# A two-layer sequence kernel: the scan stage's products in parts of two passes, new slot tables, and the conditioning work inside layer 0 of the first batch

## The reference

```
# layer 0: linear attention, 16 heads of 32, masked keys and values
q, k, v = LN(x) @ Wq, Wk, Wv;  q = softmax(q over features);  k = softmax(k over tokens)
y = q @ (k^T v)
scale, shift = silu(c) @ film_emb_W + film_emb_b          # 8x1024 @ 1024x1024
x = x + silu(LN(y) * (1 + scale) + shift) @ film_out_W
# layer 1: attention and a state-space scan side by side
shift, scale, gate = silu(c) @ W_ada + b_ada              # 8x1024 @ 1024x1536
xm = LN(x) * (1 + scale) + shift
attn = softmax attention(xm), 8 heads of 64, @ Wproj
xr, z = xm @ W_in;  u = silu(causal conv of xr, 4 taps)
dt, Bm, Cm = u @ W_x;  delta = softplus(dt @ W_dt)
h = exp(delta * A) * h + delta * u * Bm  (16 states, 1024 channels, over 512 tokens);  y = sum(h * Cm)
ssm = ((y + u * D) * silu(z)) @ W_out
out = x + gate * silu(LN([ssm, attn]) @ W_full + b_full)
```

## Time and profile before

| | us |
|---|---|
| median of 3 runs | 3960.05 (3959.69 to 3961.09) |
| the profiled execution's own time | 3962.71 |
| its span | 3960.8 |
| `setup` up to the next block's first instruction | 75.21 |
| layer 0 and attention, all batches, and the scan stage's first front | to the first scan at 1621.50 |
| 16 halves, of 140.3 (first) and 146.4 (second) in the middle | 1627.20 to 3876 |
| the last tail | to 3960.8 |

### The profile page before, as it was taken

The page is one execution under the profiler, slowest core; times in us unless marked ns, Lnnn a source line. Parts: engine busy times, 40 slices in busy tenths (PEclk is TensorE's granted clock), DMA queues, the critical chain, the costliest instruction groups (busy, mean ns, idle before and its releaser), DMA issues.

```text
span 3960.8 us, 36362 instructions
## 1 busy us (share of the span) xinstructions
PE 3387.0 (86%) x12362; PEld 1788.0 (45%) x12362; DVE 2718.3 (69%) x3459; ACT 2029.8 (51%) x3486; POOL 1893.9 (48%) x1139
## 2 busy tenths in 40 slices
PE   4899999999999998769888878888888888888758
PEld 1444444444444433444544544544544444544443
DVE  1344435344443533699898898997997997998992
ACT  1234343343433433846755755755765766676542
POOL 0021222212122211867667767766767766766661
PEclk8999999999999999668898898898898898888859
DMA  5001010100101010112122131222132122221111
GB/s 204 35 1 46 1 45 1 46 28 18 46 1 45 1 75 31 46 32 78 64 91 83 58 111 59 85 96 72 61 99 70 65 95 72 66 92 61 41 61 43
DMA packets 100937, 230.04 MB, mean 58 GB/s; under 512 B 10305, under 2 KB 10417, under 8 KB 97682
## 3 DMA queue, kind: packets, MB, share of 16 engines
q1 hardware_dynamic: 97186, 220.50, 16.5%
q10 hardware_dynamic: 3568, 7.21, 0.5%
HBM read 193.85 MB, written 33.83 MB: 57 GB/s over the span
## 4 chain that ended last, share of the span: by engine, by line
PE 18%; POOL 14%; DVE 14%; issue 13%; ACT 3%; DMA 0%; POOLq 0%; SPq 0%; DVEq 0%; ACTq 0%
POOL HS L1144 10%; PE bank L1505 10%; DVE HS L1383 6%; DVE acc L1388 5%; PE bank L1581 4%; PE bank L1522 3%; PE bank L1579 1%; DVE U L1420 1%; POOL delta L1159 1%; POOL ZS L1150 1%; ACT bank L1221 1%; POOL DU L1162 1%; POOL comb L1175 1%; PE bank L1531 0%; DVE G L1408 0%
## 5 line engine op out<-in xcount | busy, mean ns | idle before, releaser
L1144 POOL TENSOR_TENSOR HS<-DU,brep 128x1024 f32<-128x1024 f32 x512 | 1196.6, 2354 | 635.8 <-PE bank L1522 635.8
L1383 DVE TENSOR_TENSOR_SCAN HS<-bank,HS 128x1024 f32<-128x1024 f32 x512 | 1169.2, 2284 | 70.6 <-ACT bank L1221 58.0
L1522 PE MATMUL bank<-ident,HS 128*128 128x128 f32 x4096 | 686.8, 319 | 340.4 <-DVE acc L1388 305.4
L1221 ACT ACTIVATE bank<-delta,aneg 128x511 f32<-128x511 f32 x1024 | 662.0, 680 | 500.7 <-DVE HS L1383 498.6
L1522 PEld LDWEIGHTS bank<-ident,HS 128*128 128x128 f32 x4096 | 558.4, 164 | 616.3 <-DVE HS L1383 399.9
L446 POOL TENSOR_TENSOR PR<-PR,rrec 128x512 f32<-128x512 f32 x256 | 260.0, 1039 | 1128.6 <-DVE rrec L691 1128.6
L1388 DVE SCALAR_TENSOR_TENSOR acc<-bank,C,acc 128x512 f32<-128x512 f32 x960 | 668.4, 740 | 134.0 <-PE bank L1522 132.4
L1505 PE MATMUL bank<-XM,w_l 128*128 128x512 f32 x1024 | 499.8, 636 | 43.9 <-DVE U L1420 19.1
L1505 PE MATMUL bank<-w_l,G 128*128 128x512 f32 x1024 | 474.4, 609 | 7.3 <-ACT delta L1231 3.9
L523 ACT ACTIVATE PR<-bank,nsmax 128x512 f32<-128x512 f32 x256 | 173.5, 682 | 374.4 <-DVE nsmax L687 374.4
L757 PE MATMUL bank<-w_l,NT 128*128 128x512 f32 x768 | 342.6, 595 | 5.1 <-ACT NT L477 5.1
(11 more groups left out here) (169 smaller groups left out, 3877.8 us busy)
## 6 DMA issues: line engine op xcount, KB each, us to landing
brep<-b_d SPq DMA_DIRECT2D x256, 256.0 KB, 3.2
w_l<-in_L_cond_W_in SPq DMA_DIRECT2D x14, 2048.0 KB, 9.7
w_l<-in_L_cond_W_full SPq DMA_DIRECT2D x8, 2048.0 KB, 8.6
w_l<-in_L_cond_W_out SPq DMA_DIRECT2D x7, 2048.0 KB, 9.0
X<-in_x SPq DMA_DIRECT2D x8, 1024.0 KB, 5.2
x_d<-X SPq DMA_DIRECT2D x8, 1024.0 KB, 4.6
xm_d<-XM SPq DMA_DIRECT2D x8, 1024.0 KB, 3.9
ot_d<-OT SPq DMA_DIRECT2D x8, 1024.0 KB, 5.8
```

Source lines behind the costliest of these rows:

```text
L1144: nc.gpsimd.tensor_tensor(HS[:, u % DEEP], DU[:, chunks(j, s), :], brep[:, m % 3, :].unsqueeze(1).to_broadcast([P, UC, T]), ALU.mult).then ...
L1221: last = nc.scalar.activation(dA[:, s, i, 1:T], delta[:, c, 1:T], ACT.Exp, scale=aneg[:, c, n:n + 1])
L1383: nc.vector.tensor_tensor_scan(h, dA[:, u % 2].rearrange("p i t -> p (i t)"), h, 0.0, ALU.mult, ALU.add).then_inc(scanned, 1)
L1522: last = nc.tensor.transpose(y_bank[t % 2][:, i * P:(i + 1) * P], h, ident[:])
```

## The change

One part: `setup` is gone. Its loads, products and row arithmetic stand in `attend`; the first load is now X. The two conditioning weights come in five pieces of 2 MB, which lie in rooms that layer 1 uses later; `conditioning(g)` issues their products, adds and turns after chosen half-steps of batch 0's layer 0. Weights are waited for one by one. GpSimd's copy of a batch's row of `per_batch` is gone; the row is read in place.

The other part: in `mix` each product is taken up in parts of two matmuls, each with a slot of its own in tuples (`PE_XR = ((0, 0), (2, 2), ...)`: both parts of x0 at slot 0, of x1 and of x2 at slot 2), and all tables have new numbers.

```diff
-            setup(nc, a, bank, ident, cols, bq8, aneg, convw, per_batch, gate_d, X, load, arrived)
-            attend(nc, a, bank, ident, cols, col, bq8, per_batch, x1_d, xm_d, ot_d, X, W, load, load_wide, arrived)
+            attend(nc, a, bank, ident, cols, col, bq8, aneg, convw, per_batch, gate_d, x1_d, xm_d, ot_d, X, W, load, load_wide, arrived)
...
+        room = [PR[:, 0].rearrange("p e t k -> p (e t k)"), PR[:, 1].rearrange("p e t k -> p (e t k)"), QK.rearrange("p i c t -> p (i c t)"),
+                wqkv.rearrange("p c n -> p (c n)")[:, 0:EC * D]]
+        piece = [room[j % 4].rearrange("p (c n) -> p c n", n=D) for j in range(5)]
...
+        row_bank, turn_bank = bank[6:8], (bank[5], bank[4])
...
+        PE_PIECE, PE_ROWS = (14, 15, 19, 20, 21), (18, 26)
+        DVE_PIECE, DVE_ROWS = (15, 16, 20, 21, 22), (19, 27)
...
+        def l0_alone(l0, conditioning=None):
             for g in range(SLOTS):
-                l0(n, g)
+                l0(0, g)
+                if conditioning:
+                    conditioning(g)
...
+                def load_piece(j):
+                    w, k = ("L0_cond_film_emb_W", j) if j < 2 else ("L1_cond_W_ada", j - 2)
+                    sp.dma_start(piece[j], a[w][:, k * D:(k + 1) * D].rearrange("(c p) n -> p c n", p=P)).then_inc(piece_in[j], 16)
+
+                sp.dma_start(X[:], a["x"][0].rearrange("(t p) d -> p t d", p=P)).then_inc(x_in, 16)
+                for name, first, n in VECTORS:
+                    src = a[name][first:first + n * P].rearrange("(c p) -> c p", p=P)
+                    sp.dma_start(vecrows[COL[name]:COL[name] + n, :], src).then_inc(vec_in, 16)
+                sp.dma_start(maskrows[:], a["mask_BxS_ik0"].rearrange("b (t p) -> (b t) p", p=P)).then_inc(rows_in, 16)
                 load_mask(0)
+                for name in ("L0_cond_Wk", "L0_cond_Wq", "L0_cond_Wv"):
+                    load(sp, name).then_inc(arrived[name], 16)
+                load_piece(0)
+                load_piece(1)
+                load(sp, "L0_cond_film_out_W").then_inc(arrived["L0_cond_film_out_W"], 16)
+                load_piece(2)
+                load_piece(3)
+                sp.wait_ge(cond_mm, 1)
+                load_piece(4)
+                sp.wait_ge(cond_mm, 4)
+                load(sp, "L1_cond_Wqkv").then_inc(arrived["L1_cond_Wqkv"], 16)
+                sp.wait_ge(rows_done, 5)
+                sp.dma_start(gate_d, rows[4]).then_inc(gate_out, 16)
...
-                    if n:
-                        pool.wait_ge(*r0.done(n - 1, "x1", DC - 1))
-                    nc.gpsimd.tensor_copy(cur[:], per_batch[:, n, :]).then_inc(cur_done, 1)
...
+                def conditioning(g):
+                    for j in at(DVE_PIECE, g):
+                        dve.wait_ge(cond_mm, j + 1)
+                        nc.vector.tensor_tensor(rows[j], row_bank[j % 2][0:B, :], rows[j], ALU.add).then_inc(rows_done, 1)
+                    for i in at(DVE_ROWS, g):
+                        sc, sh, at_a, at_b, gain, shift, done = (
+                            (0, 1, FILM_A, FILM_B, "L0_cond_film_norm_scale", "L0_cond_film_norm_bias", film_done),
+                            (1, 0, LN1_A, LN1_B, "L1_cond_ln1_g", "L1_cond_ln1_b", ln1_done))[i]
+                        dve.wait_ge(rows_turned, i + 1)
+                        y = turn_bank[i][:, 0:2 * DC * B].rearrange("p (k c b) -> p k c b", k=2, b=B)
+                        link(nc.vector.tensor_scalar(scale1[:, i], y[:, sc], 1.0, None, ALU.add))
+                        for first, v in ((at_a, gain), (at_b, shift)):
+                            for c in range(DC):
+                                last = nc.vector.tensor_scalar(per_batch[:, :, first + c], scale1[:, i, c, :], col(v, c), None, ALU.mult)
+                        link(last)
+                        dst = per_batch[:, :, at_b:at_b + DC].rearrange("p b c -> p c b")
+                        link(nc.vector.tensor_tensor(dst, dst, y[:, sh], ALU.add))
+                        nc.vector.memset(spare[:], 0.0).then_inc(done, 1)
...
+                def conditioning(g):
+                    for j in at(PE_PIECE, g):
+                        if j == 0:
+                            pe.wait_ge(condT_done, 1)
+                        pe.wait_ge(piece_in[j], 16)
+                        if j >= 2:
+                            pe.wait_ge(rows_done, j - 1)
+                        for c in range(EC):
+                            last = nc.tensor.matmul(row_bank[j % 2][0:B, :], condT[:, c, :], piece[j][:, c, :], start=(c == 0), stop=(c == EC - 1))
+                        last.then_inc(cond_mm, 1)
+                    for i in at(PE_ROWS, g):
+                        pe.wait_ge(rows_done, 2 * i + 2)
+                        for k in range(2 * DC):
+                            src = (film, ada)[i][:, k * P:(k + 1) * P]
+                            last = nc.tensor.transpose(turn_bank[i][:, k * B:(k + 1) * B], src, ident[0:B, 0:B])
+                        last.then_inc(rows_turned, 1)
...
+        SPARED = ((), ())
...
-        PE_XR = {0: 0, 1: 1, 2: 2, 4: 3, 5: 4, 6: 5, 8: 6, 9: 7}
-        PE_Z = {10: 0, 11: 1, 14: 2, 20: 3, 22: 4, 23: 5, 25: 6, 26: 7}
-        PE_XD = {12: 0, 13: 1}
-        PE_DT1, PE_C = {15: 0, 16: 1, 18: 2, 19: 3}, 17
-        PE_O = {1: (0, 0), 2: (0, 1), 5: (1, 0), 6: (1, 1), 14: (2, 0), 15: (2, 1), 20: (3, 0), 21: (3, 1)}
-        PE_P1, PE_P0 = {29: 0, 30: 1, 31: 2}, {0: 3}
-        PE_CT = {10: (0, 0), 11: (0, 1), 16: (1, 0), 17: (1, 1), 22: (2, 0), 23: (2, 1), 27: (3, 0), 28: (3, 1)}
-        PE_F = {12: (0, 0), 13: (0, 1), 18: (1, 0), 19: (1, 1), 24: (2, 0), 25: (2, 1), 29: (3, 0), 30: (3, 1)}
-        ACT_Z = {12: 0, 14: 1, 16: 2, 23: 3, 25: 4, 26: 5, 28: 6, 29: 7}
-        ACT_P1, ACT_P0 = {30: 0, 31: 1}, {0: 2, 2: 3}
-        ACT_LN = {7: 0, 11: 1, 20: 2, 26: 3}
-        ACT_NORM = {9: 0, 13: 1, 22: 2, 27: 3}
+        PE_XR = ((0, 0), (2, 2), (2, 2), (4, 4), (5, 5), (6, 8), (8, 8), (9, 9))
+        PE_Z = ((10, 11), (11, 11), (14, 14), (20, 20), (21, 22), (23, 23), (25, 25), (26, 26))
+        PE_XD = (11, 13, 13, 13)
+        PE_DT1 = (14, 15, 15, 19)
+        PE_P = ((29, 29), (30, 31), (31, 31), (32, 32))
+        PE_O = ((1, 1, 2, 3), (5, 5, 5, 6), (14, 15, 15, 16), (20, 21, 21, 22))
+        PE_CT = ((10, 11), (17, 17), (23, 23), (28, 28))
+        PE_F = ((11, 12, 12, 13), (17, 18, 19, 19), (24, 25, 26, 26), (28, 29, 30, 31))
+        ACT_Z = {12: 0, 14: 1, 16: 2, 24: 3, 25: 4, 26: 5, 27: 6, 28: 7}
+        ACT_P = {31: 0, 32: 1, 33: 2, 35: 3}
+        ACT_LN = {8: 0, 11: 1, 20: 2, 25: 3}
+        ACT_NORM = {11: 0, 16: 1, 24: 2, 27: 3}
-        POOL_CORR1, POOL_DELTA1 = {20: 0, 22: 1, 24: 2, 26: 3}, {21: 0, 23: 1, 25: 2, 27: 3}
-        SP_B, SP_OUT, SP_OT, SP_GATE, SP_XM, SP_PROJ, SP_FULL = 16, 13, 14, 10, 1, 27, 1
+        POOL_CORR1, POOL_DELTA1 = {20: 0, 24: 1, 27: 2, 29: 3}, {22: 0, 25: 1, 28: 2, 29: 3}
+        SP_B, SP_OUT, SP_OT, SP_GATE, SP_XM, SP_PROJ, SP_FULL = 20, 17, 13, 14, 9, 23, 7
...
-                    if s in PE_F:
-                        t, k = PE_F[s]
+                    for t, k in at(PE_F, s):
                         if k == 0:
                             if t == 0:
                                 pe.wait_ge(arrived["full"], (p + 1) * 16)
                             ring.wait_free(pe, p, f"f{t}")
-                        pe.wait_ge(*ring.done(p, f"c{t}{'ab'[k]}"))
+                        pe.wait_ge(*ring.done(p, f"c{t}{'ab'[k // 2]}"))
                         last = product(ring.bank(p, f"f{t}")[:], lambda c: G[:, c, t * P:(t + 1) * P], lambda c: wide["full"][:, c, :],
-                                       range(k * HC, (k + 1) * HC), IC)
-                        if k == 1:
+                                       range(2 * k, 2 * k + 2), IC)
+                        if k == 3:
                             last.then_inc(ring.full, 1)
```

421 lines of the change are left out of this document (203 added, 218 removed).

## The result

The changed kernel takes 3943.59 us (median; 3938.46 to 3945.13) against 3960.05: a ratio of 0.9954, 95% interval 0.9938 to 0.9970. It is faster by 0.46%, 16.5 us, where I forecast 3927 and 33 us. One more execution of the changed kernel ran at a mean granted clock of 0.67 in place of 0.91, took 4820.75 us and is left out here. The time lies in the stated range of 3895 to 3953 and outside the likeliest case's own range of 3918 to 3940. It falls in the range of the rival in which the preparation hides less (3936 to 3947), but that is chance: of the 14.6 us that the span misses the forecast by, the preparation has 5.3.

The account below looks back on a forecast made before the run. VectorE was taken to pace the scan stage, TensorE a close second. Terms -40.9 - 1.9 - 17.3 + 2.8 + 19.6 + 4.1 = -33.6 us took the median from 3960.05 to 3927; range 3895 to 3953.

Parts of the forecast that it names:

- the likeliest case: Whole kernel: the forecast of 3927 us, given 55%, with its own range of 3918 to 3940.
- the rival in which the preparation hides less: Start: a late piece or a stretched layer 0 chain costs 9 to 20 us more, 3936 to 3947; chance 10%.
- The preparation: Start: transposes begin 69.3 us earlier, 28.4 of work comes back within layer 0; -40.9 us (-44 to -36).
- The lone front: Before the first scan: silu of u moved to slot 12 stops delaying the last two convolutions; -1.9 us (0 to -3).
- First halves: Scan stage, seven with a batch's tail: smaller parts cut VectorE's 0.7 waits; -2.5 us a half, -17.3 in all.
- Second halves, early: Slots 0 to 22: 3.68 at slot 21 goes, waits at slots 2, 14 and 15 come; +0.4 a half, +2.8.
- Second halves, late: Slots 23 to 31: VectorE waits 8.0 us at scan 29, mostly covered by a P product; +2.8 a half, +19.6.
- the late row: Second halves: B's row queues behind Wproj's load, moved to slot 23, delaying GpSimd, ScalarE's decay and VectorE 6.4 to 10.5 us.
- The rival in which the row costs nothing: Second halves: row lands within 3 us of issue, GpSimd as early as before; 3907 us (3898 to 3916); chance 20%.
- the 1.88 behind each P product: End of second halves: VectorE's 1.88 us wait following each P product was to stay.
- The tail: Last batch's tail, alone: norms 0 and 2 behind a copy and an O product, about 2 us each; +4.1 (0 to +5).
- The rule against the change: TensorE in woven halves: smaller groups make the clock swing and cost throughput; kept as rival, about 4040 us, chance 5%.

Follow-up runs that it names:

- the ninth: Changed kernel with GpSimd's corrections of chunks 2 and 3 at 26 and 27, output steps later only in the last half, normalisations earlier only in the last tail: 3902.3 us.
- the first: Changed start and `attend` of the changed kernel, with `mix` of the kernel before: 3923.6 us, ratio 0.9900.
- the eighth: Changed kernel with the second x product at slot 1, C's turn at 17, its copy at 18 and the second silu of u at 13: 3968.8 us.
- the tenth kernel: The ninth with ScalarE's second pair of logarithms at slot 23 and not 25: 3904.3 us.
- the fifth kernel: Changed kernel with GpSimd's corrections of chunks 2 and 3 at slots 26 and 27, not 27 and 29; Wproj's load stays at 23: 3914.5 us.
- the fourth kernel: Changed kernel with GpSimd's output steps at slots 37 to 40 and normalisations of tiles 0 and 2 one and two slots earlier, in all halves: 3977.4 us.
- the sixth: Changed kernel with GpSimd's corrections at slots 26 and 27 and Wproj's load back at slot 27: 3916.3 us.

## Why the forecast came out as it did

**The preparation** (-40.9, measured -35.6). The start at 19 us was right (19.66), the pieces cost their 6.87 each, and three of them filled the gap of 7.41. Most of the 5.3 us that are missing is slow products, which the sum did not have. The first products behind the turns took 15.94 us in place of 14.00; their row of durations (ns, min/median/max) has matmuls of 1191, twice 592, where the longest before was 697 (the profile's granted clock is 1.00 there, so the low clock is only read from the doubled durations):

```profile
L714 PE MATMUL bank<-NT,w_l x32: 592/592/1191, 24.2 to 39.6; 128*128 128x512 f32 x32
```

And from the second turns of H to the first layer-1 product it is 32.3 us (115.53 to 147.85), where it was 29.35 (154.05 to 183.40). Of the 3.0 more, 0.8 is the row turns among the products, as the sum had them, 0.5 a longer set of turns of H, and 1.7 the clock in these products. A window from the first to the last of them in the changed kernel, the same in the ninth, and the window before:

```profile
120.40:136.85 16.45, 16.45 (x40) 7.13 (x40) 5.39 (x17) 1.25 (x1) 0.00 (x0) 0.90 0.00 1
```

```profile
118.19:132.98 14.79, 14.79 (x40) 6.48 (x40) 5.39 (x17) 1.25 (x1) 0.00 (x0) 1.00 0.00 1
```

```profile
158.41:172.41 14.00, 14.00 (x32) 6.00 (x32) 3.86 (x6) 1.25 (x1) 0.00 (x0) 1.00 0.00 1
```

Neither loss is fixed by the code. The first products took 13.97 in three of the twelve kernels with the changed start (the first, the eighth and the ninth) and 15.6 to 16.3 in the others. The ninth had both groups fast: its first layer-1 product starts at 143.97, which is -39.4. The pieces landed in time.

**The lone front** (-1.9, measured 0.0). The 0.0 is a sum of two: the attention ahead came out 2.0 us shorter, and the front itself, from the first x product to the first scan, 2.0 us longer (85.2 against 83.3, and 83.7 to 85.2 in the other kernels with this front). The earlier silu order did bring the xd product forward, by 1.5 us counted from the first x product. The step that failed: I did not follow the logarithms. At slot 25 they stand behind two z products, and GpSimd waits the 5.41 us shown above; the tenth kernel, without that wait, has 82.7, only 0.6 under the 83.3.

**First halves** (-2.5 each, measured -2.3). Right in the main: four waits of 0.7 became one of 0.32, and the wait of slot 2 stayed (6.49) behind a slow P product. But that this product runs slow "before and after" was no fixed thing: with it fast, as in the fifth kernel, a first half is 2.7 us shorter still. The row:

```profile
2781.37 1.41 DVE L1431 SCALAR_TENSOR_TENSOR acc<-bank,C,acc 128x512 f32<-128x512 f32 x2 [0.32 <-PE bank L1563]
```

**Second halves, early** (+0.4 each). Right by its places but for one: 0.97 at slot 3, 0.64 and 1.65 at 14 and 15, but of the 3.68 at slot 21, which was to go, 1.58 stayed. VectorE's idling in these slots rose by 0.5 us on average.

**Second halves, late** (+2.8 each; with the early slots +3.2, measured +2.7). The size was right and the cause half wrong, so the right size is in part luck. The wait was foreseen at its place and in its size (8.0 taken, 7.6 found), but the late row, on which the working rested, was 1.8 of it; even with the row in time GpSimd's own order, of which I had the last state product and the correction in the same chain but not the delta step ahead of them, makes 5.8. The rival in which the row costs nothing would still have had the wait. I was also wrong that the 1.88 behind each P product stay. Of these three times 1.88, 2.2 us are left, at the end of the half, and that is why the wait did not cost more; with the wait gone (fifth kernel) 3.94 and 3.67 stand there. The 0.6 for a second P product at the low clock did not come: it took 1.98 and 1.88 for its halves in the changed kernel. In the eighth kernel, where it was slow, its first half took 3.78.

**The last half** (0, measured +4.3) had no term: the move of the output steps stands nowhere in my working. In the woven halves it costs nothing that shows (149.1 with it, 149.5 in the fourth kernel without).

**The tail** (+4.1, measured +9.2). The two waits are there, about 2 us each. That the first normalisation "now stands behind the copy" was a misreading, since it stood there before; by the order of instructions it is the LN. What was missing is the clock behind each, 5.7 us, of which the second part, 3.0, is absent in one kernel of eight.

**The rule against the change.** In the woven halves the choice of the row over the rule held: smaller groups, and a granted clock of 0.91 and 0.90 against 0.88 and 0.90. Where TensorE had single waits of 1.8 to 4 us between long groups, in the lone tail, the clock did fall (0.84 and 0.70), and the groups behind took longer. What the Trainium skill says in "TensorE: Matmul & The Clock Gate", section "A second HAM failure mode: psum-queue depth-cycling", is of frequent short idles between groups and of single matmuls that stay at full speed; no run here shows that, neither at the split nor in the tail.

## What to carry to other kernels

A long chain that stands alone gives back about half of its length when it is dissolved into other work (75 us of `setup` gave 33.6 to 39.4). A wait put into a stretch that runs alone costs its own length and can cost a stretch of low clock behind it. A table that serves both woven and lone stretches must be read in each of them: a place that is free in one holds a queue in the other, and a change of two things is best timed as two kernels before either is tuned. When a wait has two causes in one chain, work out what stays when the nearest one is gone. And when an edit gains where nothing of it was moved, look at TensorE's clock there before crediting the edit.

## What was not expected of the hardware

The clock at one and the same product can be low or high in the same program, and it repeats from half to half. In the tenth kernel's profiled execution two pairs of a second and a first half are 148.3 and 135.0 us and four are about 145.7 and 137.8, 283.3 and 283.5 together. In the first form the P product at the end of the second half is slow (6.2 us for its eight matmuls) and the one at the head of the first half fast (3.70); in the other the first is fast (5.1 to 5.3) and the last slow (5.2 to 5.5). The waits behind the products move accordingly. The fifth, the sixth and the ninth kernel have the first form in all seven pairs, and the changed kernel has both products slow, with 149.1 and 137.9. What picks the form was not settled.
